# Key decay on VectorE, silu in one ScalarE instruction, and another order of products and out-stages in a decoder layer

## The chip, the cores and the metric

One core of a Trainium2 chip runs one launch of the kernel. The metric is the device time in microseconds (us), the median of several runs. The engines work on their own instruction queues, in order, and wait for each other on semaphores: PE (TensorE, matmuls), ACT (ScalarE), DVE (VectorE), POOL (GpSimd) and SP (SyncE, which issues most DMAs).

## What is computed

A decoder layer with batch 2, 512 tokens, width 1024: linear attention with 32 heads of 128, a quantised product with a context, and a blocked feed-forward part, each with a residual and a layer norm. The change touches the attention alone:

```python
qkv = jax.nn.silu(hidden_states @ qkv_w.T)
...
scores = jnp.einsum('bhnd,bhmd->bhnm', cq, ck) * diag_decay
intra = jnp.einsum('bhnm,bhmd->bhnd', scores, cv)
inter = jnp.einsum('bhnd,bhde->bhne', cq * q_decay, kv)
kv_next = kv * block_decay + jnp.einsum('bhnd,bhne->bhde', ck * k_decay, cv)
...
gate = jax.nn.sigmoid(hidden_states @ gate_w.T)
return gate * normed @ out_w.T
```

## The kernel before

`make_plan` writes one list of steps; each engine's program walks this list and emits its own part of every step. So the order of the list is the order of every engine's queue, and nothing is reordered later.

Heads go in pairs, n = 0 to 15. For n = 1 to 14 one iteration of `main_part` holds four projections, in the order gate, q, k, v. Each is a `product_pair`: a block scheme with seven products (1 to 7) instead of eight, each of 12 matmuls of 128x512. Every fp32 operand is held as two f16 parts, high and low, and a product takes three terms (hi*hi, hi*lo, lo*hi: lines 1386, 1387, 1388). The high part is written by ACT, the low part by DVE (`split_low`, line 1740). The four results r of a projection come from bank 0 (product 2), bank 1 (product 3), bank 2 (product 4), and `p_copy` (products 5 and 7, joined by the addition `c22`, line 1791). `u3` (line 1788) joins products 6 and 7 in bank 2 ahead of products 4 and 5; product 3 waits for `c22`; `seed` (line 1617) copies bank 0 into bank 1 ahead of product 2.

Between the products, `slots` put other work: `p6` is what follows product 6. There are the splits of the next weights (`part(0)`, `part(1)`, `part(2)`: ACT line 1601, DVE line 1740), whose sums POOL makes (`pair_sum`, lines 2026 to 2031: the sum `s1` feeds part 1, `s4` part 2); the attention of the pair before (`scores`, `attend`, `gated`); and its output projection, 16 `out_stage` steps (`stages`), also in seven products, of three matmuls each (lines 1473 to 1475), whose results DVE adds into `acc` (line 1908). Stages 0 to 3 stand in q, 4 to 11 in k, 12 to 15 in v. Stage 1 needs the block `S2`, a sum of gated units that POOL makes and ACT (line 1671) and DVE split into `gated_split`.

A `silu` step is: ACT Sigmoid into `sig` (line 1637), DVE multiply of result and `sig` (line 1801), ACT high part (line 1643), DVE low part. For the keys, results 0 and 2 are kept in `sig`; POOL multiplies them by the decay (`k_decay`, line 2047) once the low part is done; `turn_keys` splits them and SP transposes them by DMA, for the `state` product (line 1359) at the start of the next gate. The values are transposed by DMA as well (`v_turn`); their result 0 goes through the buffer `s_kt` (named `scores_keys` in the profile), which the scores' split writes as well.

## Time and profile before

| | us |
|---|---|
| median of 3 runs | 1957.35 (1956.63 to 1958.7) |
| the profiled execution, its own time | 1958.86 |
| its span in the profile | 1957.0 |
| PE busy in the span | 1804.3 |
| DVE busy | 1474.8 |
| ACT busy | 927.7 |
| POOL busy | 705.5 |

The span runs from the first to the last instruction of one execution; its own time is 1.9 us longer. Matmuls are pipelined, so that the busy time of PE counts overlapping instructions once; where it waits, the profile shows idle time and what ended it.

### The profile page before, as it was taken

To read this page: it belongs to the slowest core of one execution; us is meant where nothing else is said; L and a number is where in the kernel's file an instruction comes from. 1 tells how busy PE (TensorE), PEld (TensorE's weight loads), DVE (VectorE), ACT (ScalarE), POOL (GpSimd) and SP (SyncE) were. 2 spreads that over 40 slices of the span, in tenths; PEclk is the share of its full clock that TensorE was granted. 3 is DMA by queue.
4 is the path that set the end of the run, shared out by engine and by line. 5 is a ranking of instruction groups with operands and counts; after the bars stand their busy time and mean duration, and the time that the engine had idled before them with its cause. 6 is when DMAs were issued, how large, how long until landed. Compare 5 with 4: busy or idle time off the path is not lost.

```text
span 1957.0 us, 27828 instructions
## 1 busy us (share of the span) xinstructions
PE 1804.3 (92%) x9865; PEld 892.1 (46%) x9865; DVE 1474.8 (75%) x2029; ACT 927.7 (47%) x1402; POOL 705.5 (36%) x536
## 2 busy tenths in 40 slices
PE   7899899999999999999999998999999998998887
PEld 4354434445454544435454444445453444565332
DVE  7777777868777777878776777868677777768877
ACT  5554444545454444545444444445444454434674
POOL 3253333344433343344333333444333433301433
PEclk9999999999999999999999999999999999999998
DMA  5223323131423223131321213131231313233322
GB/s 183 61 65 99 69 87 102 65 102 44 129 60 97 71 87 102 61 102 49 114 75 58 78 54 83 51 93 56 70 69 50 103 54 81 76 100 116 108 87 87
DMA packets 158119, 161.54 MB, mean 83 GB/s; under 512 B 99872, under 2 KB 127904, under 8 KB 157600
## 3 DMA queue, kind: packets, MB, share of 16 engines
q1 hardware_dynamic: 146528, 147.09, 25.6%
q0 software_dynamic: 2560, 8.39, 1.3%
q10 hardware_dynamic: 8896, 4.28, 0.8%
q8 instruction: 82, 1.34, 0.3%
q14 instruction: 53, 0.43, 0.1%
HBM read 123.56 MB, written 12.58 MB: 70 GB/s over the span
## 4 chain that ended last, share of the span: by engine, by line
DVE 42%; PE 19%; issue 13%; ACT 12%; DMA 9%; POOL 4%; SPq 1%; ACTq 0%; DVEq 0%; POOLq 0%
DVE w_pair L1740 7%; DVE acc L1908 5%; DVE gated_split L1740 5%; DVE scores_keys L1740 4%; PE bank L1386 4%; PE bank L1387 4%; PE bank L1388 4%; DMA decay_sb<-rates 3%; DMA v_split<-scores_keys 3%; DVE w_vo L1740 3%; DVE bank L1801 3%; PE bank L1359 3%; ACT w_pair L1601 3%; ACT sig L1637 2%; DVE p_copy L1791 2%
## 5 line engine op out<-in xcount | busy, mean ns | idle before, releaser
L1386 PE MATMUL bank<-x_blocks,w_pair 128*128 128x512 f16 (+1 forms) x1820 | 684.8, 376 | 33.0 <-DVE p_copy L1791 17.6
L1387 PE MATMUL bank<-x_blocks,w_pair 128*128 128x512 f16 (+1 forms) x1820 | 683.5, 376 | 0.0
L1388 PE MATMUL bank<-x_blocks,w_pair 128*128 128x512 f16 (+1 forms) x1820 | 682.4, 375 | 0.0
L1386 PEld LDWEIGHTS bank<-x_blocks,w_pair 128*128 128x128 f16 x1820 | 179.4, 99 | 246.6 <-DVE p_copy L1791 24.8
L1388 PEld LDWEIGHTS bank<-x_blocks,w_pair 128*128 128x128 f16 x1820 | 179.4, 99 | 206.8 <-issue 7.2
L1387 PEld LDWEIGHTS bank<-x_blocks,w_pair 128*128 128x128 f16 x1820 | 179.4, 99 | 190.5 <-issue 7.0
L1740 DVE SCALAR_TENSOR_TENSOR w_pair<-raw_pair,w_pair 128x1024 f16<-128x1024 f32 x126 | 183.4, 1475 | 54.4 <-ACT w_pair L1601 54.2
L1908 DVE TENSOR_TENSOR acc<-acc,bank 128x512 f32<-128x512 f32 x320 | 206.6, 677 | 13.9 <-PE bank L1475 13.9
L2047 POOL TENSOR_TENSOR sig<-sig,decay_sb 128x512 f32<-128x512 f32 x30 | 38.2, 1272 | 474.2 <-DVE k_units L1740 474.2
L1473 PE MATMUL bank<-w_vo,gated_split 128*128 128x512 f16 x392 | 151.6, 387 | 62.0 <-DVE acc L1908 47.9
L2057 POOL TENSOR_TENSOR ssq<-ssq,sig 128x512 f32<-128x512 f32 x64 | 81.9, 1279 | 268.7 <-ACT sig L1659 268.7
L1475 PE MATMUL bank<-w_vo,gated_split 128*128 128x512 f16 x392 | 151.6, 387 | 0.0
L1474 PE MATMUL bank<-w_vo,gated_split 128*128 128x512 f16 x392 | 151.2, 386 | 0.0
L1740 DVE SCALAR_TENSOR_TENSOR scores_keys<-bank,scores_keys 128x256 f16<-128x256 f32 (+1 forms) x176 | 89.1, 543 | 81.0 <-ACT scores_keys L1651 42.0
L1601 ACT ACTIVATE w_pair<-raw_pair 128x1024 f16<-128x1024 f32 x126 | 129.1, 1049 | 43.6 <-POOL raw_pair L2027 43.6
L2026 POOL TENSOR_TENSOR sums_pair<-raw_pair 128x512 f32<-128x512 f32 x63 | 100.8, 1600 | 113.3 <-DVE w_pair L1740 93.7
L1637 ACT ACTIVATE sig<-bank 128x512 f32<-128x512 f32 x145 | 85.8, 592 | 114.0 <-PE bank L1388 74.0
L1740 DVE SCALAR_TENSOR_TENSOR gated_split<-k_units,gated_split 128x512 f16<-128x512 f32 x98 | 123.3, 1269 | 9.7 <-ACT gated_split L1671 9.7
L1740 DVE SCALAR_TENSOR_TENSOR w_pair<-sums_pair,w_pair 128x1536 f16<-128x1536 f32 x63 | 110.4, 1753 | 1.9 <-ACT w_pair L1601 0.7
L1651 ACT ACTIVATE scores_keys<-bank 128x512 f16<-128x512 f32 (+1 forms) x132 | 58.6, 491 | 111.8 <-DMA v_split<-scores_keys 74.7
L1659 ACT ACTIVATE sig<-bank 128x512 f32<-128x512 f32 x64 | 38.2, 597 | 149.1 <-DVE bank L1879 147.0
L1601 ACT ACTIVATE w_pair<-sums_pair 128x1536 f16<-128x1536 f32 x63 | 93.0, 1475 | 30.0 <-POOL sums_pair L2031 30.0
(220 smaller groups left out, 2849.6 us busy)
## 6 DMA issues: line engine op xcount, KB each, us to landing
raw_pair<-w_qk SPq DMA_DIRECT2D x32, 1024.0 KB, 5.6
raw_pair<-w_gate SPq DMA_DIRECT2D x16, 1024.0 KB, 5.0
raw_pair<-w_out SPq DMA_DIRECT2D x16, 1024.0 KB, 5.1
raw_pair<-w_vt SPq DMA_DIRECT2D x15, 1024.0 KB, 4.9
raw_pair<-ctx_in SPq DMA_DIRECT2D x8, 1024.0 KB, 4.9
decay_sb<-rates SPq DMA_DIRECT2D x60, 128.0 KB, 4.5
acc<-x_t SPq DMA_DIRECT2D x4, 1024.0 KB, 11.2
ctx<-raw_pair SPq DMA_DIRECT2D x8, 512.0 KB, 3.9
```

The costliest lines, as they stand in the source:

```text
L1386: pe.matmul(out, w_hi, x_hi, start=unmet and k == 0, stop=False, skip_group_check=halves or not fresh)
L1387: pe.matmul(out, w_hi, x_lo, start=False, stop=False, skip_group_check=halves or not fresh)
L1388: mm = pe.matmul(out, w_lo, x_hi, start=False, stop=k == QT - 1, skip_group_check=halves or not fresh)
L1473: pe.matmul(out, g_hi, w_hi, start=fresh, stop=False, skip_group_check=not fresh)
L1474: pe.matmul(out, g_hi, w_lo, start=False, stop=False, skip_group_check=not fresh)
L1475: pe.matmul(out, g_lo, w_hi, start=False, stop=True, skip_group_check=not fresh).then_inc(sem["out_mm"])
L1601: act.activation(hi, src, ACT.Copy, scale=W_SCALE).then_inc(sem["w_hi"])
L1637: act.activation(c.sig32[st["gi"]][:, :], src, ACT.Sigmoid, scale=st["sign"] / W_SCALE).then_inc(sem["sig"])
L1740: return dve.scalar_tensor_tensor(out=lo, in0=src, scalar=scale, in1=hi, op0=ALU.mult, op1=ALU.subtract)
L1908: dve.tensor_tensor(dst, dst, bank, ALU.add).then_inc(sem["acc"])
L2026: pool.tensor_tensor(s3, a11, a21, ALU.add)
L2057: pool.tensor_tensor(c.ssq[:, b], c.ssq[:, b], c.sig32[st["gi"]][:, :], ALU.add).then_inc(sem["ssq"])
```

## The change

1. The decay of the keys, `k_decay`, is made by DVE instead of POOL, and stands in the list as a step of its own: `decay(0)` in k between `stages(8)` and `part(1)`, `decay(1)` after `part(0)` at the end of k.
2. `silu` is one ACT instruction, `ACT.Silu`, from the bank into `sig`; both splits read `sig`; DVE's multiply is gone. A bank is released once ACT has read it. Gate keeps Sigmoid.
3. In q, product 7 stands ahead of 6, `gate(3)` and `gate(2)` come right behind the last attention, the q result of product 2 behind stage 0, and unit 3 and `S2` are split behind it. In v, the order is 1, 7, 6, 4, 2, 5, 3, the stages 14 and 15 stand behind 6 and 4, and the scores behind 5. The values' result 2, made by product 4, goes through `s_kt` in place of result 0.

```diff
@@ -85,7 +85,7 @@
 FIRST = {
     "before": "x0 v0 t1 v1 l x2 p00 t3 p10 x1 p11 p01 x3 w0 t2 p02 w2 p12 x5 p03",
     "q": {"p1": "x6 x4 w1 e00", "p7": "l", "p6": "w0 w1 p13 w2", "p4": "l", "p3": "w0"},
-    "k": {"p1": "e10", "p6": "w1 w2 l", "p5": "j0", "p3": "c w0 j1"},
+    "k": {"p1": "e10", "p6": "w1 w2 l d0", "p5": "j0", "p3": "d1 c w0 j1"},
     "gate": {"p2": "e01 e11", "p6": "s0", "p5": "g0", "p4": "w1 w2", "p3": "l g2 g3 g1"},
 }
...
@@ -326,33 +326,29 @@
         self.gate_done[r // 2] = self.tick("gate_sig")
         self.release(place, self.gate_done[r // 2])
-    def silu(self, done, place, sign, dst, dst_free, kept=False):
+    def silu(self, done, place, sign, dst, dst_free):
         gi = self.sig_at % 2
         self.sig_at += 1
-        st = self.add("silu", done=done, place=place, sign=sign, gi=gi, sig_free=self.sig_free[gi], sig=self.tick("sig"),
-                      silu=self.tick("silu"), dst=dst, free=dst_free if isinstance(dst_free, list) else [dst_free],
-                      slot=self.late_slot, hi=self.tick("qkv_hi"), kept=kept)
-        self.sig_free[gi] = st["silu"]
-        self.kept = gi, st["silu"]
-        return self.tick("qkv_lo")
+        st = self.add("silu", done=done, place=place, sign=sign, gi=gi, sig_free=self.sig_free[gi], silu=self.tick("silu"),
+                      dst=dst, free=dst_free if isinstance(dst_free, list) else [dst_free], slot=self.late_slot,
+                      hi=self.tick("qkv_hi"))
+        lo = self.sig_free[gi] = self.tick("qkv_lo")
+        return gi, st["silu"], lo
     def qk_out(self, which, r):
         done, place, sign = self.result(r)
-        decayed = which == "k" and r % 2 == 0
-        lo = self.silu(done, place, sign, (which, r), [self.qk_free, self.g_split] if which == "k" else
-                       [self.qk_free, self.q_read], decayed)
-        if decayed:
-            gi, silu = self.kept
-            self.release(place, silu)
-            self.decay_keys(r // 2, gi, lo)
-        else:
-            self.release(place, lo)
+        gi, silu, lo = self.silu(done, place, sign, (which, r), [self.qk_free, self.g_split] if which == "k" else
+                                 [self.qk_free, self.q_read])
+        self.release(place, silu)
+        if which == "k" and r % 2 == 0:
+            self.kd[r // 2] = gi, lo
         for b in range(B):
             self.qk_done[(which, r // 2, b)] = lo
-    def decay_keys(self, g, gi, lo):
+    def decay_keys(self, g):
+        gi, lo = self.kd[g]
         self.add("k_decay", g=g, gi=gi, lo=lo, rate=self.rate_ready[g])
         rate = self.rate_free[g] = self.sig_free[gi] = self.tick("k_rate")
         self.kd[g] = gi, rate
...
@@ -387,11 +383,11 @@
     def v_out(self, r):
         done, place, sign = self.result(r)
-        lo = self.silu(done, place, sign, ("v_unit", r), self.s_free if r == 0 else self.vo_free)
-        self.release(place, lo)
+        _, silu, lo = self.silu(done, place, sign, ("v_unit", r), self.s_free if r == 2 else self.vo_free)
+        self.release(place, silu)
         self.add("v_turn", r=r, ready=lo, free=max(self.v_hl_free))
         self.v_turned[r] = self.tick(f"v_turned{r}", 16)
-        if r == 0:
+        if r == 2:
             self.s_free = self.v_turned[r]
         if r == 1:
             self.v_done = [[self.v_turned[2:], self.v_turned[:2]] for _ in range(B)]
...
@@ -806,7 +802,7 @@
             plan.add_c22()
         if i in (6, 7) and {6, 7} <= met:
             plan.add_u3()
-        if i in (2, 5, 4, 3):
+        if i in (2, 5, 4, 3) and i not in put_off:
             out({2: 0, 5: 3, 4: 2, 3: 1}[i])
         fill(f"p{i}")
...
@@ -962,12 +961,12 @@
             "p4": [part(1)],
             "p3": [part(2)],
         } if last else {
-            "p1": [attend(3), gated(3)] + units(3),
-            "p2": sums(S2) + split_sum(S2) + stages(0) + sums(S1),
-            "p6": stages(1) + split_sum(S1) + sums(S4) + gate_rest + split_sum(S4),
-            "p7": stages(2) + [part(0), part(1)],
+            "p1": [attend(3), gated(3)] + gate_rest,
+            "p2": sums(S2) + stages(0) + [lambda: plan.qk_out("q", 0)] + units(3) + split_sum(S2) + sums(S1),
+            "p7": stages(1) + split_sum(S1) + sums(S4) + split_sum(S4),
+            "p6": stages(2) + [part(0), part(1)],
             "p3": stages(3) + [part(2)],
-        }, (1, 2, 6, 7, 5, 4, 3))
+        }, (1, 2, 6, 7, 5, 4, 3) if last else (1, 2, 7, 6, 5, 4, 3), put_off=() if last else (2,))
         plan.load_decay(n * GH, last)
         plan.load_decay(n * GH + 1, last)
         if last:
...
@@ -977,18 +976,19 @@
             "p1": stages(4) + stages(5) + ([stash] if stashing else []),
             "p7": stages(6),
             "p2": stages(7),
-            "p6": [part(0)] + stages(8) + [part(1)] + stages(9),
+            "p6": [part(0)] + stages(8) + [decay(0), part(1)] + stages(9),
             "p5": stages(10) + [part(2)] + [turn(0)],
             "p4": stages(11),
-            "p3": [part(0)],
+            "p3": [part(0), decay(1)],
         })
         plan.load_rates(n, "q")
         product_pair(plan, "v", n, {
             "p1": stages(12) + [turn(1), part(1)],
             "p7": stages(13) + [part(2)],
-            "p2": stages(14),
-            "p6": stages(15) + [lambda: plan.scores(n, UNITS[0])],
-        }, (1, 7, 2, 6, 4, 5, 3))
+            "p6": stages(14),
+            "p4": stages(15),
+            "p5": [lambda: plan.scores(n, UNITS[0])],
+        }, (1, 7, 6, 4, 2, 5, 3))
 def final_part(plan):
...
@@ -1631,12 +1631,12 @@
             until(act, sem, st["free"])
             act.activation(c.sig32[st["gi"]][:, :], c.banks[st["bank"]][:, :], ACT.Copy).then_inc(sem["v_copied"])
         elif kind == "silu":
-            src = c.placed(st["place"])
             act.wait_ge(sem[st["done"][0]], st["done"][1])
             until(act, sem, st["sig_free"])
-            act.activation(c.sig32[st["gi"]][:, :], src, ACT.Sigmoid, scale=st["sign"] / W_SCALE).then_inc(sem["sig"])
+            act.activation(c.sig32[st["gi"]][:, :], c.placed(st["place"]), ACT.Silu,
+                           scale=st["sign"] / W_SCALE).then_inc(sem["silu"])
+            src = c.sig32[st["gi"]][:, :]
             act.wait_ge(sem["silu"], st["silu"][1])
-            src = c.sig32[st["gi"]][:, :] if st["kept"] else src
             for token in st["free"]:
                 until(act, sem, token)
             for cols, (dst, _) in c.split_targets(st):
...
@@ -1795,12 +1795,7 @@
             dve.wait_ge(sem["v_mm"], st["mm"][1])
             dve.tensor_tensor(bank[:, :], c.sig32[st["gi"]][:, :], bank[:, :], ALU.subtract).then_inc(sem["v_sub"])
         elif kind == "silu":
-            src = c.placed(st["place"])
-            dve.wait_ge(sem["sig"], st["sig"][1])
-            out = c.sig32[st["gi"]][:, :] if st["kept"] else src
-            dve.scalar_tensor_tensor(out=out, in0=src, scalar=st["sign"] / W_SCALE, in1=c.sig32[st["gi"]][:, :],
-                                     op0=ALU.mult, op1=ALU.mult).then_inc(sem["silu"])
-            src = out
+            src = c.sig32[st["gi"]][:, :]
             dve.wait_ge(sem["qkv_hi"], st["hi"][1])
             for cols, (hi, lo) in c.split_targets(st):
                 ins = split_low(like(src[:, cols], lo), 1.0, hi, lo)
...
@@ -1859,6 +1854,11 @@
+        elif kind == "k_decay":
+            k = c.sig32[st["gi"]][:, :].rearrange("p (b s) -> p b s", b=B)
+            dve.wait_ge(sem["qkv_lo"], st["lo"][1])
+            until(dve, sem, st["rate"])
+            dve.tensor_tensor(k, k, c.rate(st["g"], B), ALU.mult).then_inc(sem["k_rate"])
```

What this does to the queues, at three places. ACT at the start of q: the rows of before, then of the changed kernel. `k_units` holds the gated units here, `p_copy` and the banks the gate results. L1671 splits a unit or sum, L1676 is the seed of an out-stage.

```order
-L1637 ACTIVATE sig_0<-bank 128x512
-L1643 ACTIVATE q_units<-bank 128x2x256
-L1671 ACTIVATE gated_split<-k_units 128x512
-L1676 ACTIVATE bank<-bank 128x512
-L1671 ACTIVATE gated_split<-k_units 128x512
-L1627 ACTIVATE gate_units<-p_copy 128x2x256
-L1627 ACTIVATE gate_units<-bank 128x2x256
```

```order
+L1627 ACTIVATE gate_units<-p_copy 128x2x256
+L1627 ACTIVATE gate_units<-bank 128x2x256
+L1676 ACTIVATE bank<-bank 128x512
+L1636 ACT_TABLE_LOAD
+L1636 ACTIVATE sig_0<-bank 128x512
+L1643 ACTIVATE q_units<-sig_0 128x2x256
+L1671 ACTIVATE gated_split<-k_units 128x512 x2
```

Both gate results and the seed moved ahead, a table load stands before the first silu of q, and the splits of unit 3 and `S2` moved behind it. The other load of an iteration stands ahead of `gate(0)`.

POOL in k, before: four sums of a weight pair (here the k weights'), the decay, and the sums of the v weights, then the second decay.

```order
L2031 TENSOR_TENSOR sums_pair<-raw_pair,sums_pair 128x512
L2047 TENSOR_TENSOR sig_0<-sig_0,decay_sb 128x512
L2026 TENSOR_TENSOR sums_pair<-raw_pair 128x512
L2027 TENSOR_TENSOR raw_pair<-raw_pair 128x512
L2029 TENSOR_TENSOR sums_pair<-raw_pair 128x512
L2031 TENSOR_TENSOR sums_pair<-raw_pair,sums_pair 128x512
L2047 TENSOR_TENSOR sig_0<-sig_0,decay_sb 128x512
```

In the changed kernel the two rows with `decay_sb` are gone from POOL and the sums follow each other. DVE in k has the first of them, now line 1861, between the splits of `part(0)` and `part(1)`:

```order
L1788 TENSOR_TENSOR bank<-bank,p_copy 128x512
L1740 SCALAR_TENSOR_TENSOR w_pair<-raw_pair,w_pair 128x1024
L1908 TENSOR_TENSOR acc<-acc,bank 128x512
L1861 TENSOR_TENSOR sig_0<-sig_0,decay_sb 128x512
L1740 SCALAR_TENSOR_TENSOR w_pair<-raw_pair,w_pair 128x1024
L1908 TENSOR_TENSOR acc<-acc,bank 128x512 x2
L1791 TENSOR_TENSOR p_copy<-bank,p_copy 128x512
```

Before, the same rows stood there without the line 1861.

## Rows read from the trace of the kernel before

**Rows 1.** The page, busy time of each engine over the span.

```profile
PE 1804.3 (92%) x9865; PEld 892.1 (46%) x9865; DVE 1474.8 (75%) x2029; ACT 927.7 (47%) x1402; POOL 705.5 (36%) x536
```

**Rows 2.** The waits of PE: us in total, times, longest.

```profile
PE bank L1473 <- DVE acc L1908: 47.9, 40, 2.6
PE bank L1386 <- DVE p_copy L1791: 17.6, 14, 2.6
```

**Rows 3.** Windows: length, busy us of PE, PEld, DVE, ACT, POOL, then clock, DMA.

```profile
599.50:660.66 61.16, 56.36 (x256) 24.54 (x255) 44.14 (x57) 26.89 (x38) 20.59 (x14) 0.97 0.40 112
660.66:688.37 27.71, 27.71 (x205) 17.18 (x205) 23.02 (x34) 15.15 (x25) 10.04 (x8) 1.00 0.18 48
688.37:710.09 21.72, 20.60 (x96) 8.79 (x94) 17.45 (x23) 10.62 (x18) 11.41 (x8) 1.00 0.14 49
```

**Rows 4.** Timeline of PE: last product of v, first product and state of gate.

```profile
654.52 0.39 PE L1386 MATMUL bank<-x_blocks,w_pair 128*128 128x512 f16 x1 [0.92 <-DVE p_copy L1791]
654.74 0.38 PE L1387 MATMUL bank<-x_blocks,w_pair 128*128 128x512 f16 x1
...
660.66 0.83 PE L1359 MATMUL bank<-v_split,scores_keys 128*128 128x128 f16 x12 [0.79 <-DMA v_split<-w_vo]
```

**Rows 5.** Timeline: the stall in the k product, 604 to 627 us; its first and last kin.

```profile
177.93 0.39 PE L1473 MATMUL bank<-w_vo,gated_split 128*128 128x512 f16 x1 [2.59 <-DVE acc L1905]
...
604.27 0.37 SPq L1319 DMA_DIRECT2D raw_pair<-w_vt  x1
614.38 1.28 POOL L2047 TENSOR_TENSOR sig<-sig,decay_sb 128x512 f32<-128x512 f32 x1 [22.81 <-DVE k_units L1740]
619.18 1.06 ACT L1601 ACTIVATE w_pair<-raw_pair 128x1024 f16<-128x1024 f32 x1 [3.12 <-POOL raw_pair L2027]
621.44 1.27 DVE L1908 TENSOR_TENSOR acc<-acc,bank 128x512 f32<-128x512 f32 x2
622.77 0.39 PE L1473 MATMUL bank<-w_vo,gated_split 128*128 128x512 f16 x1 [2.60 <-DVE acc L1908]
...
623.75 0.63 PE L1473 MATMUL bank<-w_vo,gated_split 128*128 128x512 f16 x1
...
626.31 0.48 PE L1386 MATMUL bank<-x_blocks,w_pair 128*128 128x512 f16 x1
...
1621.29 0.39 PE L1473 MATMUL bank<-w_vo,gated_split 128*128 128x512 f16 x1 [2.59 <-DVE acc L1908]
```

**Rows 6.** The page, DMA issues: KB each, median us to landing.

```profile
raw_pair<-w_vt SPq DMA_DIRECT2D x15, 1024.0 KB, 4.9
```

**Rows 7.** Timeline of DVE, ACT, POOL and PE, end of gate to q.

```profile
680.65 0.68 DVE L1740 SCALAR_TENSOR_TENSOR gated_split<-k_units,gated_split 128x512 f16<-128x512 f32 x1
...
690.23 0.75 DVE L1888 SCALAR_TENSOR_TENSOR k_units<-bank,norm_w_sb,gate_units 128x512 f32<-128x512 f32 x1 [0.75 <-ACT sig L1659]
...
691.50 4.36 POOL L2053 TENSOR_TENSOR k_units<-k_units 128x512 f32<-128x512 f32 x3
...
695.21 1.21 DVE L1740 SCALAR_TENSOR_TENSOR gated_split<-k_units,gated_split 128x512 f16<-128x512 f32 x1
695.63 0.39 PE L1473 MATMUL bank<-w_vo,gated_split 128*128 128x512 f16 x1 [0.62 <-ACT bank L1676]
```

**Rows 8.** Groups of DVE instructions: busy us, mean ns, idle before.

```profile
L1801 DVE SCALAR_TENSOR_TENSOR bank<-bank,sig 128x512 f32<-128x512 f32 x115 | 79.5, 691 | 17.8 <-ACT sig L1637 17.7
L1801 DVE SCALAR_TENSOR_TENSOR p_copy<-p_copy,sig 128x512 f32<-128x512 f32 x47 | 33.6, 714 | 32.7 <-ACT sig L1637 32.7
L1801 DVE SCALAR_TENSOR_TENSOR sig<-bank,sig 128x512 f32<-128x512 f32 x30 | 20.7, 692 | 47.4 <-ACT sig L1637 47.4
```

**Rows 9.** Timeline of ACT around a table load, product q of block 0.

```profile
38.89 1.04 ACT L1601 ACTIVATE w_pair<-raw_pair 128x1024 f16<-128x1024 f32 x1
39.95 1.28 ACT L1637 ACT_TABLE_LOAD   x1
41.25 0.60 ACT L1637 ACTIVATE sig<-bank 128x512 f32<-128x512 f32 x1
```

More of the change, by code:

```diff
@@ L66 @@
 SEMAPHORES = (
-    ["const_in", "ones_set", "constants", "quant_set", "x_hi", "x_lo", "w_hi", "w_lo", "sig", "silu", "qkv_hi", "qkv_lo",
+    ["const_in", "ones_set", "constants", "quant_set", "x_hi", "x_lo", "w_hi", "w_lo", "silu", "qkv_hi", "qkv_lo",
      "gate_sig", "score_mm", "decayed", "s_hi", "s_lo", "attend_mm", "sq", "gated", "g_sum", "g_hi", "g_lo", "ssq", "out_mm", "out_seeded",
@@ L250, in split_vo @@
         self.add("vo_split", part=part, slot=item["slot"], ready=item["landed"], late=late, out=item["what"][0] == "o",
-                 free=[max(self.first_mm.values())] if late else [self.vo_free] + self.v_turned[1:], hi=self.tick("w_hi"))
+                 free=[max(self.first_mm.values())] if late else [self.vo_free, self.v_turned[0], self.v_turned[1], self.v_turned[3]], hi=self.tick("w_hi"))
         lo = self.tick("w_lo")
@@ L270, in split_wo @@
         ready = (item["t1"], item["t1"], item["t4"])[part]
-        self.add("wo_split", part=part, slot=item["slot"], ready=ready, free=[self.vo_free] + self.v_turned[1:],
+        self.add("wo_split", part=part, slot=item["slot"], ready=ready, free=[self.vo_free, self.v_turned[0], self.v_turned[1], self.v_turned[3]],
                  hi=self.tick("w_hi"))
@@ L378, in kv_out @@
         done, place, sign = self.result(r)
-        lo = self.silu(done, place, sign, ("kv", b, r), [self.qk_free, self.g_split, self.late_units_free])
-        self.release(place, lo)
+        _, silu, lo = self.silu(done, place, sign, ("kv", b, r), [self.qk_free, self.g_split, self.late_units_free])
+        self.release(place, silu)
         self.qk_done[("k", r // 2, b)] = lo
@@ L424, in end_v @@
         bank = v["banks"][half]
-        done = self.silu(v["mm"][half], bank, 1.0, ("v", v["b"], half), self.v_hl_free[v["b"]])
+        _, silu, done = self.silu(v["mm"][half], bank, 1.0, ("v", v["b"], half), self.v_hl_free[v["b"]])
         self.v_done[v["b"]] = [[done]] * GH
-        self.main_ring.give(bank, done)
+        self.main_ring.give(bank, silu)
     def values(self, b):
@@ L929, in state, with decay @@
             return lambda: plan.state(g)
+        def decay(g):
+            return lambda: plan.decay_keys(g)
         def turn(g):
@@ L1160, in __init__ @@
         self.g32 = {unit: k_flat[:, unit * D:(unit + 1) * D].bitcast(F32) for unit in UNITS}
-        self.v_units = [self.s_kt[:, 0:2 * S]]
-        self.v_units += [vo_flat[:, i * 2 * S:(i + 1) * 2 * S] for i in range(3)]
+        self.v_units = {r: vo_flat[:, i * 2 * S:(i + 1) * 2 * S] for i, r in enumerate((0, 1, 3))}
+        self.v_units[2] = self.s_kt[:, 0:2 * S]
         self.hid += [self.g[:, i].rearrange("p n s -> p (n s)").bitcast(F32) for i in range(4)]
```

11 lines of the change are left out of this document (3 added, 8 removed).

## The prediction

> **What bounds the kernel now.** I read the busy times first. PE works 1804 of 1957 us, DVE 1475 [rows 1], so TensorE is the engine to keep fed, and DVE the one that most often fails to feed it. The waits of PE say where: out-products wait for DVE's additions into `acc` (47.9 us in 40 waits, the longest 2.6), and products for DVE's `c22` addition (17.6 us) [rows 2]. Everything repeats with n, 14 times (n = 1 to 14), so I cut one iteration into stretches: from the first product of k to the first product of the next gate 61.16 us, the rest of gate with its attention 27.71 us, and q up to its last out-product 21.72 us, together 110.6 us [rows 3]. The gate stretch has PE busy all through.
>
> How much of the other two is stall? Two products start 0.22 us apart when nothing waits (654.52 and 654.74 [rows 4]); I use 0.216. The k/v stretch holds 15 products of 12 and 21 out-products of 3 matmuls, 243 x 0.216 = 52.5 us, and 12 short score matmuls (2304 columns in each of their three terms' sum, about 1.0 us): 53.5 of 61.2, so 7.7 us per iteration are stalls and slow matmuls. The q stretch holds 72 + 21 matmuls, 20.1 of 21.7 us: 1.6 us of stalls.
>
> The large stall is that of the out-stage behind product 5 of k: PE waits 2.60 us for `acc` at 622.77, and the same stands at 177.93 first and 1621.29 last, once in each of the 14 iterations [rows 5]. Followed back: the addition (621.44) stands on DVE behind the low split of the v weights' part 1; that waits for ScalarE's high split (619.18), which waited 3.12 us for POOL's sum `raw_pair` L2027. POOL was late because it works in program order and the k decay (614.38) stood ahead of the sums: it had waited 22.81 us for the split of the keys, then took 1.28 us. The v weights had been asked for at 604.27; such a load lands in 4.9 us, at 609.2 [rows 5, 6]. POOL lost 6.4 us (609.2 to 615.66) that nothing in the data required.
>
> Behind this stall the matmuls last 0.63 instead of 0.38 us (623.75, still 0.48 at 626.31 [rows 5]), and the granted clock of the stretch reads 0.97 while the other two have 1.00 [rows 3]: the engine fell from 2.4 to 1.2 GHz for some eight matmuls after idling 2.6 us, 8 x 0.21 = 1.7 us. Two smaller waits end the stretch: product 3 of v 0.92 us for `c22`, the state product 0.79 us for the transposed values [rows 4].
>
> **The change, part by part.**
>
> *Decay to DVE.* Removes the POOL instruction above; POOL's sums can start at landing. In the times of the trace: sums from 609.2, each 1.28 alone, so s1 at 611.8 and s4 at 614.4, ahead of every user. ScalarE's part 1 then follows part 0 and the seed, at 616.1 to 617.2, instead of 620.2. DVE: `u3` to 615.5, part 0 to 616.7, one addition to 617.4, the decay to 618.1 (no row shows it on DVE; the two-input split of the same shape is 0.68 with POOL idle, 1.21 beside POOL [rows 7]; POOL is idle here, so 0.7), part 1 to 619.3, two additions to 620.5. PE is ready at 620.2 (622.77 less its wait): the stall shrinks from 2.6 to 0.5, and the half-clock matmuls go. The second decay frees POOL the same way for the sums of the gate weights. These sums feed the splits behind which the additions of stage 13 stand, on which stage 14 waits. Of the 47.9 us in [rows 2] 13 waits of 2.6 are the stall above (the first of the 14 waited for a copy, L1905); the other 27 share 14 us, 1 us per iteration, and should mostly go.
>
> *Silu in one instruction.* Removes DVE's multiply: 115 + 47 + 30 = 192 instructions, 133.8 us of DVE [rows 8], 0.7 us from the chain of each of the 12 results per iteration, and with it a handshake ScalarE to DVE and back. ScalarE's own count stays; Silu is in no row; Sigmoid of this shape is 0.60 (41.25 [rows 9]) and so is Square, whose end starts gated at 690.23 [rows 7]. An activation of 1024 columns lasts 1.04 [rows 9], so 512 columns lie between half of that and 0.60: I take 0.60. But the low split now reads `sig` in SBUF instead of a bank: 0.68 alone, 1.21 beside POOL [rows 7]. POOL is busy a third of the time [rows 1], so of 12 splits some 4 lose 0.5 us: 8.4 saved and about 2 + 2 x 0.7 given back, net 5 us of DVE per iteration.
>
> *Table loads.* Gate still uses Sigmoid, so each iteration loads a table twice: ahead of gate(0) and ahead of the first q silu, 30 more in all. The trace shows one between two activations: previous end 39.93, load 39.95 to 41.23, next 41.25 [rows 9]: 1.28 us plus the 0.1 by which activations otherwise overlap, 1.38. The Trainium skill (ScalarE: Activation LUTs, What ACT_TABLE_LOAD costs) prices a switch at 1.28 us of load and 1.38 us of drain, 2.66 in all; this row shows no such drain, and I go by the row. By the skill's figure each of the two places would be some 1.3 us later and the time 1926 + 14 x 2.6 = 1962 us.
>
> *v products reordered, scores behind product 5.* The scores (1.0 us of PE) now stand between product 5 and product 3, which waits for `c22`: that covers the 0.92 us. Also the values that go through the scores' buffer come from product 4 before the scores, and their transpose is over when the scores are split; ScalarE no longer stands behind it. New risk: product 4 follows product 6 with one out-stage between (1.3 us), and `u3` on DVE stands behind stage 13's additions and a 1.75 us split; I work out 0.6 us of stall. The state product needs v's transposes; their chain is a multiply and a handshake shorter (about 0.75 us) and PE arrives sooner: 0.3 us of wait left.
> Sum for k/v: 0.5 + 0.6 + 0.3 and 0.3 of small seed waits = 1.7 us of stall against 7.7: gain 6.0. Low end: only the 2.6 us stall and the `c22` wait go, 3.5; high end 7.
>
> *q reordered.* Here the change costs. Cut the chain at the last attend of the iteration, whose matmuls end at 688.37. First, the load ahead of gate(0) sits in front of the split of S3 and of an out-weight part, for which DVE works without slack, so DVE's join and ScalarE's work reach attend 3 about 1.3 us later; the seed of q then ends at 689.2 and product 2, ahead of which it had half a us to spare, starts 0.9 us late. gated(3), 690.23 to 690.98 [rows 7], becomes 692.3. ScalarE next has gate(3), gate(2), the out seed (3 x 0.6, to 694.0), the load, silu and high split of q (2.6, to 696.5); only then the high splits of unit 3 and of S2. DVE behind it: low splits of q, unit 3 and S2. In the trace such a split beside POOL lasts 1.21 (695.21, POOL busy from 691.50 [rows 7]), and POOL will be busy: 3 x 1.21, to 700.1. PE arrives at S2's product at 696.4 (product 2, stage 0, product 7, three matmuls). Stall 3.7 us; with 0.68 per split it is 2.1. Before, S2 was ready at 696.4, and PE stalled 0.62 there (695.63). So stalls of 3.7 + 0.9 = 4.6 against 1.6: loss 3.0. What follows (`u3`, stage 2, the splits) I find covered. And a 3.7 us idle may drop the clock as the 2.6 us one does, 1.7 us; it did so in part of the iterations, so I charge half, 0.8.
>
> **Sum.** 6.0 - 3.0 - 0.8 = 2.2 us per iteration, 14 x 2.2 = 31 us; start and end, with 2 loads and a few shorter chains, about nothing. The profiled execution took 1958.9 us with a span of 1957.0; the median of the runs is 1957.35, which the forecast starts from: 1926 us.
>
> **Rivals.**
> - *S2's split decides (slower).* Place: stage 1 of q. The row shows a load behind an idle-free copy, not one between PSUM reads of other tables. Bounded from above by two loads' length in each place (2 x 1.28), and with the clock dropping each time, the loss is 3.0 + 2 x 1.28 + 1.7 = 7.3 against 6.0: +1.3 x 14 = +18, 1975 us. It decides from a loss of 6 us per iteration in q. For it: a load and three splits in a row ahead of one product. Against: the gap of 0.02 us behind the load [rows 9]. Chance 0.2. (The Trainium skill's drain, cited above, is this mechanism.)
> - *The gain stays at the stall itself.* DVE is busy 44 of 61 us in the stretch [rows 3]; if the next stall takes over there (stage 14, or product 4 behind `u3`), k/v gains 3.5, all that q costs (3.8): 1957 to 1961. Chance 0.15.
> - *q is cheap.* Splits at 0.68 and the gate's load absorbed: the stall at S2 is 1.7, no more than q has now; no clock drop: 14 x 5.9 = 83, 1875 us. Against: POOL works all through that place. Chance 0.2.
> - *My sum*, own range 1905 to 1945: chance 0.45.
>
> **How the numbers follow.** A measurement of this kernel tells some 0.2% (4 us) from no change. Faster: 0.45 + 0.2 and a part of the second rival, 0.7. Same 0.08. Slower 0.22. The range leaves out half of the cheap case's far end and half of the slow one's: 1882 to 1970.
>
> **What would show it.** Right: the 2.6 us waits of out-products for `acc` in k are gone; POOL's sums begin at landing; DVE's busy time falls by about 70 to 100 us; no wait of product 3 of v; a new wait of PE in q for the low split of `gated_split`, 2 to 4 us, 14 times; table loads of 1.28 us. Wrong: if that q wait is above 6 us or absent, or if the k stall remains with another releaser (then the late sums were not its cause). The forecast fails most easily in q, where I placed eight instructions from durations taken in another order.

## The result: 16 us faster, half of what was forecast

| | before | after |
|---|---|---|
| median, us | 1957.72 (4 runs) | 1941.45 (1940.58 to 1946.51, 4 runs) |
| ratio, 95% interval | | 0.9922 (0.9905 to 0.994) |
| profiled execution, its span | 1958.86, 1957.0 | 1941.43, 1939.6 |

The forecast was 1926 us, a gain of 31; 1941.45 lies in its range of 1882 to 1970, and the gain of 16 is about half of it.

The page of the profile after, busy time of each engine, to be set beside [rows 1]:

```profile
PE 1808.5 (93%) x9865; PEld 896.1 (46%) x9865; DVE 1383.3 (71%) x1867; ACT 975.0 (50%) x1432; POOL 641.9 (33%) x506
```

DVE has 91.5 us less to do, ACT 47 us more, most of it the 30 table loads (30 x 1.28 = 38). PE has the same matmuls and is busy 4 us longer although the span is 17 us shorter: some of them have become slow. The waits of PE (total, times, longest), to be set beside [rows 2]:

```profile
PE bank L1473 <- issue: 54.5, 14, 3.9
PE bank L1386 <- DVE bank L1788: 12.1, 15, 0.8
...
PE bank L1386 <- ACT gate_units L1627: 5.0, 12, 0.4
...
PE bank L1359 <- DVE k_units L1888: 4.7, 12, 0.4
...
PE bank L1473 <- DVE acc L1908: 0.6, 3, 0.2
```

The two rows of before have all but gone: out-products wait 0.6 us in all for this addition into `acc`, never more than 0.2, and `c22` holds up one product in all. In their place stands one wait, 14 times 3.9 us. "issue" means that no releaser is shown; the timeline finds it below. The three stretches of one iteration, cut as in [rows 3] but in time order k/v, gate, q:

```profile
595.72:651.19 55.47, 54.47 (x257) 24.18 (x256) 40.49 (x49) 26.36 (x37) 16.14 (x12) 1.00 0.41 123
651.19:679.56 28.37, 27.97 (x204) 17.09 (x205) 22.60 (x33) 17.01 (x26) 10.03 (x8) 1.00 0.20 48
679.56:707.27 27.71, 23.37 (x96) 9.66 (x95) 16.14 (x21) 12.21 (x19) 11.24 (x8) 0.88 0.11 39
```

k/v gave 5.7 us (61.16 before), gate lost 0.7 (27.71), q lost 6.0 (21.72). The clock reads 1.00 where it was 0.97, and 0.88 in q, where it was 1.00.

**k.** POOL, DVE and PE in the timeline, where [rows 5] had the 2.60 us stall:

```profile
604.68 1.27 POOL L2026 TENSOR_TENSOR sums_pair<-raw_pair 128x512 f32<-128x512 f32 x1 [21.22 <-DMA raw_pair<-w_vt]
...
613.35 0.69 DVE L1861 TENSOR_TENSOR sig<-sig,decay_sb 128x512 f32<-128x512 f32 x1
613.95 1.22 DVE L1740 SCALAR_TENSOR_TENSOR w_pair<-raw_pair,w_pair 128x1024 f16<-128x1024 f32 x1
615.09 1.28 DVE L1908 TENSOR_TENSOR acc<-acc,bank 128x512 f32<-128x512 f32 x2
...
616.42 0.39 PE L1473 MATMUL bank<-w_vo,gated_split 128*128 128x512 f16 x1
```

POOL's first sum now waits for its load (DMA), no longer for a decay; the decay costs DVE 0.69 us; the out-stage starts without a wait.

**q.** ACT, DVE, POOL and PE of the same iteration:

```profile
684.49 1.28 ACT L1636 ACT_TABLE_LOAD   x1
685.78 0.60 ACT L1636 ACTIVATE sig<-bank 128x512 f32<-128x512 f32 x1
686.41 0.63 ACT L1643 ACTIVATE q_units<-sig 128x512 f16<-128x512 f32 x1
686.95 1.13 ACT L1671 ACTIVATE gated_split<-k_units 128x512 f16<-128x512 f32 x2
...
687.07 0.85 DVE L1740 SCALAR_TENSOR_TENSOR q_units<-sig,q_units 128x512 f16<-128x512 f32 x1 [2.73 <-ACT q_units L1643]
687.85 3.42 DVE L1740 SCALAR_TENSOR_TENSOR gated_split<-k_units,gated_split 128x512 f16<-128x512 f32 x2
...
687.34 1.71 POOL L2026 TENSOR_TENSOR sums_pair<-raw_pair 128x512 f32<-128x512 f32 x1
...
687.07 0.38 PE L1475 MATMUL bank<-w_vo,gated_split 128*128 128x512 f16 x1
691.38 0.58 PE L1473 MATMUL bank<-w_vo,gated_split 128*128 128x512 f16 x1 [3.92 <-issue]
...
692.61 0.63 PE L1386 MATMUL bank<-x_blocks,w_pair 128*128 128x512 f16 x1
693.03 0.63 PE L1387 MATMUL bank<-x_blocks,w_pair 128*128 128x512 f16 x1
```

DVE idled 2.73 us for the chain load, silu, high split. Then it made the low splits of q, of unit 3 and of `S2`, the last two at 1.7 us each with POOL at work (whose own sum lasts 1.71 instead of 1.27). They end at 691.27 and PE goes on at 691.38. Between the last start before the wait and the first behind it lie 4.31 us, 4.08 to 4.09 more than between neighbours. The profile itself gives the idle time, 3.92; a "stall" below is counted between starts, a "wait" in the profile's rows is idle time. Behind it the matmuls start 0.42 us apart (692.61, 693.03) instead of 0.216: the lower clock level, 1.2 GHz, for 13 matmuls here.

### The profile page after: what moved, and what is told of

Its sections match the earlier page's. It is cut to its first block, busy times and chain, and to the rows that moved or that the text cites. A ratio compares the mean times of both kernels' runs of the same rounds, so it can differ in the third digit from the quotient of the medians.

```text
span 1939.6 us, 27666 instructions
## 1 busy us (share of the span) xinstructions
PE 1808.5 (93%) x9865; PEld 896.1 (46%) x9865; DVE 1383.3 (71%) x1867; ACT 975.0 (50%) x1432; POOL 641.9 (33%) x506
## 4 chain that ended last, share of the span: by engine, by line
PE 54%; DVE 17%; issue 16%; ACT 9%; POOL 3%; DMA 1%; ACTq 0%; DVEq 0%; POOLq 0%; SPq 0%
PE bank L1386 13%; PE bank L1387 13%; PE bank L1388 13%; DVE w_pair L1740 4%; PE bank L1359 4%; PE bank L1473 3%; PE bank L1475 3%; PE bank L1474 2%; DVE acc L1908 2%; POOL ssq L2052 1%; ACT sig L1636 1%; DVE gated_split L1740 1%; ACT k_units L1643 1%; ACT w_pair L1601 1%; PE bank L1537 1%
## 5 line engine op out<-in xcount | busy, mean ns | idle before, releaser
L2026 POOL TENSOR_TENSOR sums_pair<-raw_pair 128x512 f32<-128x512 f32 x63 | 93.5, 1485 | 647.8 <-DVE w_pair L1740 453.5
L1908 DVE TENSOR_TENSOR acc<-acc,bank 128x512 f32<-128x512 f32 x320 | 212.0, 681 | 43.6 <-PE bank L1475 41.9
L1740 DVE SCALAR_TENSOR_TENSOR w_pair<-raw_pair,w_pair 128x1024 f16<-128x1024 f32 x126 | 170.2, 1370 | 14.0 <-ACT w_pair L1601 13.9
L1636 ACT ACTIVATE sig<-p_copy 128x512 f32<-128x512 f32 x47 | 29.6, 630 | 244.7 <-DVE p_copy L1791 244.7
L1740 DVE SCALAR_TENSOR_TENSOR k_units<-sig,k_units 128x512 f16<-128x512 f32 (+1 forms) x68 | 69.9, 1027 | 101.0 <-ACT k_units L1643 90.6
L1740 DVE SCALAR_TENSOR_TENSOR q_units<-sig,q_units 128x512 f16<-128x512 f32 x64 | 49.3, 770 | 100.8 <-ACT q_units L1643 100.8
L1740 DVE SCALAR_TENSOR_TENSOR gated_split<-k_units,gated_split 128x512 f16<-128x512 f32 x98 | 111.9, 1164 | 10.9 <-ACT gated_split L1671 10.9
L1740 DVE SCALAR_TENSOR_TENSOR w_pair<-sums_pair,w_pair 128x1536 f16<-128x1536 f32 x63 | 110.5, 1755 | 5.1 <-ACT w_pair L1601 3.8
L1740 DVE SCALAR_TENSOR_TENSOR scores_keys<-bank,scores_keys 128x256 f16<-128x256 f32 (+1 forms) x162 | 79.5, 532 | 42.6 <-ACT scores_keys L1666 22.7
```

Source lines behind the costliest of these rows:

```text
L1636: act.activation(c.sig32[st["gi"]][:, :], c.placed(st["place"]), ACT.Silu, scale=st["sign"] / W_SCALE).then_inc(sem["silu"])
L1740: return dve.scalar_tensor_tensor(out=lo, in0=src, scalar=scale, in1=hi, op0=ALU.mult, op1=ALU.subtract)
L1908: dve.tensor_tensor(dst, dst, bank, ALU.add).then_inc(sem["acc"])
L2026: pool.tensor_tensor(s3, a11, a21, ALU.add)
```

## Experiments

The first four ran beside each other (before: 1958.24 us), the next four (1958.01), then the last two (1959.21). "Changed" is the changed kernel. Where an edit adds or removes a source line, line numbers move by one to six. A line `...` stands for parts of an edit that are left out.

**decay_only.** Before, with the decay alone moved to DVE, at the two places of the change.

```diff
-            self.decay_keys(r // 2, gi, lo)
+            self.kd[r // 2] = gi, lo
...
-            "p6": [part(0)] + stages(8) + [part(1)] + stages(9),
+            "p6": [part(0)] + stages(8) + [lambda: plan.decay_keys(0), part(1)] + stages(9),
...
-            "p3": [part(0)],
+            "p3": [part(0), lambda: plan.decay_keys(1)],
...
```

> The kernel before with one edit: the decay of the keys on DVE, at the places it has in the changed kernel; silu, gate, q and v as before. Theory of the late sums (the prediction's): POOL's sums start when the v weights land, the 2.6 us wait of the out-stage behind product 5 of k falls to 0.7 us or less in all 14 iterations, and so do the half-clock matmuls behind it: 1925 us, between 1915 and 1935. Rival (DVE's load is the bound, the late sums only the place where it shows): the wait moves to the next additions, 1950 to 1958 us, DVE busy 20 us more.

Measured: 1914.23 us (1911.32 to 1916.01), ratio 0.9781 (0.9765 to 0.9798). The waits of PE:

```profile
PE bank L1474 <- DVE acc L1914: 18.0, 41, 0.7
PE bank L1387 <- DVE p_copy L1792: 16.2, 14, 2.5
```

The longest wait for `acc` fell from 2.6 to 0.7 us, the wait for `c22` stayed. One part of the change gives 44 us, more than twice what the whole gives. It is 11 us more than I expected, 1 us outside the range; from the first iteration to the last the timeline holds no half-clock matmuls, where before has 80 (17 us).

**q_split_first.** Changed, with unit 3 and `S2` split ahead of q's first result and its table load; all loads stay.

```diff
-            "p1": [attend(3), gated(3)] + gate_rest,
-            "p2": sums(S2) + stages(0) + [lambda: plan.qk_out("q", 0)] + units(3) + split_sum(S2) + sums(S1),
+            "p1": [attend(3), gated(3)] + gate_rest + units(3),
+            "p2": sums(S2) + split_sum(S2) + stages(0) + sums(S1) + [lambda: plan.qk_out("q", 0)],
```

> The changed kernel with one edit in q: the splits of unit 3 and S2 stand ahead of the out seed, and the q result of product 2 (with the table load) behind them. Theory of the order in q: the 4.1 us wait of the S2 out-product falls to 1 us or less, and with it the matmuls at half clock behind it (8 to 13 of them, 1.7 to 2.8 us): 4 to 6 us per iteration, 1941 to 1857 to 1885 us. Rival (something else holds the iteration at 110.4 us, for example the weight loads and POOL's sums, so that PE waits elsewhere): 1925 us or more, with a new wait in k or v of the size of the one removed.

Measured: 1891.68 us (1887.85 to 1892.65), ratio 0.9659 (0.964 to 0.9678). The waits of PE:

```profile
PE bank L1386 <- DVE bank L1788: 23.1, 29, 0.8
PE bank L1473 <- DVE acc L1908: 13.6, 15, 1.0
```

The 3.9 us wait and every half-clock matmul of the iterations are gone: 50 us by the place of two steps. It is 7 us short of the expected range. The 14 iterations alone gave 56 us, 4.0 each, the low end of what I expected, since two waits follow: stage 2 now waits 1.0 us for `acc`, behind the q split and its load, and product 5 waits 0.8 us for `u3` in q, as a product in v does. Start and end together took 6 us more than in the changed kernel's profile.

**gate_silu.** Changed, with gate through Silu too, so that no table is switched in an iteration. Its gate values are not the reference's.

```diff
-            act.activation(dst, like(c.placed(st["place"]), dst), ACT.Sigmoid,
+            act.activation(dst, like(c.placed(st["place"]), dst), ACT.Silu,
```

> The changed kernel with the gate computed by the Silu function instead of Sigmoid (so the gate values are others than the reference's), which leaves no table load in the loop; everything else is the same. Theory that both loads lie on the chain to S2: the wait of the S2 out-product falls from 4.1 to about 1.5 us, the seed of q is 1.3 us earlier, together 2.7 us per iteration and part of the half-clock matmuls: 1890 to 1905 us. Rival (the loads are hidden and only the order of the splits counts): 1935 to 1941 us. If a switch costs the 2.66 us that the Trainium skill states (ScalarE: Activation LUTs, What ACT_TABLE_LOAD costs), the wait would vanish altogether and ACT's idle time would fall by as much again as its loads.

Measured: 1896.85 us (1894.38 to 1899.2), ratio 0.9693 (0.9674 to 0.9713). The waits of PE:

```profile
PE bank L1473 <- issue: 34.9, 14, 2.5
```

Two loads (2.6 us of ACT) per iteration are worth 45 us, 3.2 per iteration, in this order: 1.4 us of the `S2` wait, the gate's waits, and 89 of 126 half-clock matmuls (89 x 0.21 = 19 us). These stand behind only 5 of the 14 waits now, 7 or 8 at a time; in the other 9 iterations a new stall of 0.74 us for `u3` in q takes a part back.

**multiply_back.** Changed, with Sigmoid and DVE's multiply again: no loads in an iteration, and 192 multiplies. The product always goes into `sig` in SBUF, so that the splits read `sig` as in the changed kernel, not a bank as before.

```diff
...
-            act.activation(c.sig32[st["gi"]][:, :], c.placed(st["place"]), ACT.Silu,
+            act.activation(c.sig32[st["gi"]][:, :], c.placed(st["place"]), ACT.Sigmoid,
...
+            dve.wait_ge(sem["sig"], st["sig"][1])
+            dve.scalar_tensor_tensor(out=src, in0=c.placed(st["place"]), scalar=st["sign"] / W_SCALE, in1=src,
+                                     op0=ALU.mult, op1=ALU.mult).then_inc(sem["silu"])
...
```

> The changed kernel with silu undone alone: Sigmoid by ScalarE into sig, DVE's multiply of the result and sig into sig; the decay on DVE and all orders stay as changed, no table loads in the loop. DVE gets 192 multiplies of 0.69 us back (133 us). Theory (silu's gain on DVE is mostly hidden in this order, its loads are not): the wait for S2 loses 1.4 us of load and gains about 0.8 us of multiply and handshake, the gate part gains 1.3 us: 1920 to 1935 us, faster than the changed kernel. Rival (the single-instruction silu is where the gain came from): 1960 us or more.

Measured: 1970.37 us (1964.36 to 1975.52), ratio 1.0058 (1.0034 to 1.0082). The waits of PE, then DVE in q:

```profile
PE bank L1473 <- issue: 55.0, 14, 3.9
PE bank L1473 <- DVE acc L1911: 17.1, 27, 0.8
...
PE bank L1359 <- DMA v_split<-w_vo: 11.2, 14, 1.0
```

```profile
698.94 0.69 DVE L1800 SCALAR_TENSOR_TENSOR sig<-bank,sig 128x512 f32<-128x512 f32 x1
700.32 1.53 DVE L1740 SCALAR_TENSOR_TENSOR q_units<-sig,q_units 128x512 f16<-128x512 f32 x1 [0.69 <-ACT q_units L1643]
701.78 3.42 DVE L1740 SCALAR_TENSOR_TENSOR gated_split<-k_units,gated_split 128x512 f16<-128x512 f32 x2
```

My expectation fell, and the time is the rival's. The chain to `S2` lost the load's 1.28 us and got the multiply (0.69) and a q split of 1.53 instead of 0.85: the same wait. So Silu with its loads is worth 29 us in this order and 74 without them (gate_silu), and what a load costs depends on what would stand in its place in that chain.

**decay_back.** Changed, with the decay on POOL again, right behind the key result.

```diff
             self.kd[r // 2] = gi, lo
+            self.decay_keys(r // 2)
...
-            "p6": [part(0)] + stages(8) + [decay(0), part(1)] + stages(9),
+            "p6": [part(0)] + stages(8) + [part(1)] + stages(9),
...
```

> The changed kernel with the decay alone undone: it runs on POOL again, directly behind the key result, as before. Theory of the late sums: POOL's sums of the v weights wait for the keys again, PE waits 2 to 3 us for acc behind product 5 of k in every iteration, with half-clock matmuls behind it: 2.5 to 4 us per iteration, 1975 to 1995 us. Rival (in the new order the sums have slack, and the move was worth something only before): 1941 to 1950 us.

Measured: 2016.03 us (2009.53 to 2020.6), ratio 1.0303 (1.028 to 1.0325). Its timeline, POOL, ACT and PE in k:

```profile
745.51 1.27 POOL L2043 TENSOR_TENSOR sig<-sig,decay_sb 128x512 f32<-128x512 f32 x1 [27.27 <-DVE k_units L1741]
750.30 1.06 ACT L1602 ACTIVATE w_pair<-raw_pair 128x1024 f16<-128x1024 f32 x1 [2.39 <-POOL raw_pair L2023]
...
753.89 0.39 PE L1474 MATMUL bank<-w_vo,gated_split 128*128 128x512 f16 x1 [1.86 <-DVE acc L1904]
```

The chain of [rows 5] is back link by link, with late sums; its wait is 1.9 us, less than the 2 to 3 expected, and no half-clock matmuls stand behind it. With it come waits in v of up to 2.4 us for `u3` (33.9 us in 16, start included), and half-clock matmuls behind these and behind the wait for `S2`. The decay is worth 75 us in this order, 21 more than I expected at most.

**v_back.** Changed, with the order of v (products, stages, scores, and the values' buffer) as before.

```diff
...
-            "p6": stages(14),
-            "p4": stages(15),
-            "p5": [lambda: plan.scores(n, UNITS[0])],
-        }, (1, 7, 6, 4, 2, 5, 3))
+            "p2": stages(14),
+            "p6": stages(15) + [lambda: plan.scores(n, UNITS[0])],
+        }, (1, 7, 2, 6, 4, 5, 3))
...
```

> The changed kernel with v alone undone: products in the order 1, 7, 2, 6, 4, 5, 3, stages 14 and 15 and the scores behind 2 and 6, result 0 through the scores' buffer. Theory: the waits of product 3 for c22 (0.9 us) and of the state product for the transposes (0.8 us, less 0.7 for the shorter chain) return, and the 0.97 us wait of product 4 for u3 goes: +0 to +1 us per iteration, 1941 to 1955 us. Rival (the order of v carries the gain of k and v): 1970 us or more.

Measured: 1949.1 us (1947.23 to 1949.67), ratio 0.9951 (0.9935 to 0.9968). The wait of product 3 for `c22` is back (16.0 us in 15 waits). The new order of v is worth 8 us, as expected.

**q_back.** Changed, with the order of q as before. Its results are then read in two groups with gate's between them, so that it loads four tables per iteration instead of two.

```diff
-            "p1": [attend(3), gated(3)] + gate_rest,
-            "p2": sums(S2) + stages(0) + [lambda: plan.qk_out("q", 0)] + units(3) + split_sum(S2) + sums(S1),
-            "p7": stages(1) + split_sum(S1) + sums(S4) + split_sum(S4),
-            "p6": stages(2) + [part(0), part(1)],
+            "p1": [attend(3), gated(3)] + units(3),
+            "p2": sums(S2) + split_sum(S2) + stages(0) + sums(S1),
+            "p6": stages(1) + split_sum(S1) + sums(S4) + gate_rest + split_sum(S4),
+            "p7": stages(2) + [part(0), part(1)],
...
-        }, (1, 2, 6, 7, 5, 4, 3) if last else (1, 2, 7, 6, 5, 4, 3), put_off=() if last else (2,))
+        }, (1, 2, 6, 7, 5, 4, 3))
```

> The changed kernel with q alone undone: products 1, 2, 6, 7, 5, 4, 3, S2 split ahead of stage 0, gate(3) and gate(2) behind stage 1. That puts Sigmoid between silus, so an iteration loads a table four times, not twice (58 loads in the loop). Theory (order, not loads, makes the long stall): the 4.1 us wait and its half-clock matmuls go (6.5 us), two more loads of 1.38 us and the old waits of q (1.6 us) come, at worst all in PE's way: 1941 - 14 x 6.5 + 14 x 4.4 = 1911 us, between 1885 and 1925. Rival (loads are what costs): 1950 us or more.

Measured: 1894.59 us (1890.82 to 1895.74), ratio 0.9677 (0.9661 to 0.9693). The page and the waits:

```profile
PE 1787.4 (95%) x9865; PEld 888.1 (47%) x9865; DVE 1393.1 (74%) x1867; ACT 1012.8 (54%) x1460; POOL 647.6 (34%) x506
```

```profile
PE bank L1386 <- DVE bank L1788: 14.9, 29, 0.8
PE bank L1473 <- ACT bank L1676: 10.7, 13, 0.9
PE bank L1473 <- issue: 9.4, 14, 0.7
PE bank L1386 <- ACT gate_units L1627: 9.4, 14, 0.7
```

With twice the loads (ACT 38 us busier) it is 47 us faster than the changed kernel, inside the expected range, and has no half-clock matmuls in the iterations. The new order of q is the one part of the change that costs, and it costs 47 us.

**u3_first.** q_split_first, with two DVE splits moved behind `u3`: S4's in q, and the gate weights' last part in v.

```diff
-            "p7": stages(1) + split_sum(S1) + sums(S4) + split_sum(S4),
-            "p6": stages(2) + [part(0), part(1)],
+            "p7": stages(1) + split_sum(S1) + sums(S4),
+            "p6": split_sum(S4) + stages(2) + [part(0), part(1)],
...
-            "p7": stages(13) + [part(2)],
-            "p6": stages(14),
+            "p7": stages(13),
+            "p6": [part(2)] + stages(14),
```

> q_split_first with two more moves: the split of S4 behind u3 in q, and part(2) of the gate weights behind u3 in v. Both u3 additions are then the next thing DVE does when product 6 ends; PE waits 0.95 and 0.97 us for them in every iteration of q_split_first. Theory (each wait is local): 1.5 to 1.9 us less per iteration, 1892 to 1866 to 1873 us. Rival (106.65 us per iteration, which q_split_first and gate_silu share to 0.05 us, is set by a chain beside PE): the waits move, 1886 to 1892 us.

Measured: 1859.73 us (1857.03 to 1861.57), ratio 0.9495 (0.9479 to 0.9511). The waits for `u3` went. The 14 iterations gave 27.1 us, which is the two waits of 0.96 us x 14; the other 4 to 5 us lie outside the iterations, and take the total 6 us below the expected range.

**units_first.** Changed, with only unit 3's split moved ahead of q's first result; `S2`'s stays behind it.

```diff
-            "p1": [attend(3), gated(3)] + gate_rest,
-            "p2": sums(S2) + stages(0) + [lambda: plan.qk_out("q", 0)] + units(3) + split_sum(S2) + sums(S1),
+            "p1": [attend(3), gated(3)] + gate_rest + units(3),
+            "p2": sums(S2) + stages(0) + [lambda: plan.qk_out("q", 0)] + split_sum(S2) + sums(S1),
```

> The changed kernel with only the split of the last gated unit moved ahead of the gate results, so that it no longer waits behind the Silu load; S2's own split stays behind q's first result. My theory: stage 1's wait shrinks from 4.08 us to between 2 and 3 us, and what the shorter stall saves is its own 1 to 2 us in each iteration and, on top, part of the half-clock matmuls behind it, since stalls of 2.7 us had them in 5 to 9 of 14 places and stalls of 4.08 us in 13 of 14: 1941 - 14 x (1.5 + 0.8) = 1909 us, 1897 to 1922. Rival: the clock has no part in it and only the wait counts, 1941 - 14 x 1.5 = 1920 us, with as many half-clock places as before. Second rival: the Silu load ahead of q's first split sets the end of the wait anyway, stall of 3.5 us or more and 1932 us or above.

Measured: 1918.38 us (1917.17 to 1919.87), ratio 0.9792 (0.9776 to 0.9809). The wait of stage 1 in the timeline of PE:

```profile
682.34 0.38 PE L1473 MATMUL bank<-w_vo,gated_split 128*128 128x512 f16 x1 [2.64 <-issue]
682.55 0.38 PE L1474 MATMUL bank<-w_vo,gated_split 128*128 128x512 f16 x1
```

The total lies by the first rival (1920), but by the accounts of the next section its condition is not met: from the first state product to the last, the 14 iterations took 1516.27 us against 1546.35, 30.1 less. The wait went from 4.08 to 2.80 us: 14 x 1.28 = 17.9. Half-clock matmuls went from 126 to 62: 64 x 0.211 = 13.5. Together 31.4. Waits that moved with them bring it to 30.0: `u3` in q is waited for in 5 iterations (0.74 us each, 3.7 more), and the two stalls of 0.56 and 0.58 us at attend 3 and at bank 2 come in 2 iterations fewer (2.3 less). The 7 us by which the whole fell short lie outside the iterations (400.3 us of the span against 393.3), where the edit changes nothing; 8 half-clock matmuls at 57 us, which the changed kernel's profile does not have there, are 1.7 of them.

**loads_later.** u3_first, with both loads of an iteration behind the work that PE waits for.

```diff
-            "p4": sums(S3) + [gate(0)] + split_sum(S3) + [wo(1), attend(2), score(3), gated(2)],
+            "p4": sums(S3) + split_sum(S3) + [wo(1), gate(0), attend(2), score(3), gated(2)],
...
-            "p2": sums(S2) + split_sum(S2) + stages(0) + sums(S1) + [lambda: plan.qk_out("q", 0)],
-            "p7": stages(1) + split_sum(S1) + sums(S4),
+            "p2": sums(S2) + split_sum(S2) + stages(0) + sums(S1),
+            "p7": stages(1) + split_sum(S1) + [lambda: plan.qk_out("q", 0)] + sums(S4),
```

> The fastest version so far (1859.7 us) with both table loads of an iteration moved behind the work that the matmuls wait for: q's first result (and its Silu load) behind stages 1 and S1's split, and the gate's first result (and its Sigmoid load) behind S3's split and the next weight part. My theory: stage 2's wait for the accumulator falls from 1.18 us to about 0.4, and the two waits of 0.55 and 0.58 us at attend 3 and at the gate's bank shrink or stay: 1859.7 - 14 x (0.8 to 1.6) = 1837 to 1849 us. Rival: a result that is read later gives its bank back later, and the wait moves to a later product of the same pair: 1857 us or above.

Measured: 1834.02 us (1833.36 to 1837.04), ratio 0.936 (0.9345 to 0.9376), the fastest of all. The page, then what is left of waits in products:

```profile
PE 1776.7 (97%) x9865; PEld 892.8 (49%) x9865; DVE 1375.3 (75%) x1867; ACT 976.3 (53%) x1432; POOL 656.1 (36%) x506
```

```profile
PE bank L1386 <- DVE bank L1788: 3.4, 12, 0.8
```

The waits for `acc`, for the gate's bank and for attend 3 are gone; an iteration takes 102.6 us on average, against 110.5. The loads are all still there, and PE hardly waits for them: of the gaps, one of 0.34 us is left in most iterations. The total is 3 us below the expected range.

## Why the prediction was right in direction and twice too large

Each profile is cut in three here; the middle part runs from the first state product of a gate (line 1359) to the fifteenth, 14 iterations apart; half-clock matmuls are those that start 0.42 us after the one before:

| | before the first | 14 iterations | behind the last | half-clock matmuls in the 14 |
|---|---|---|---|---|
| before | 105.29 | 1553.74 | 297.97 | 80, at 11 places |
| after | 100.61 | 1546.35 | 292.64 | 126, at 13 places |
| units_first | 102.23 | 1516.27 | 298.1 | 62, at 9 places |
| gate_silu | 100.53 | 1497.89 | 294.08 | 37, at 5 places |
| decay_only | 102.48 | 1507.29 | 299.7 | none |
| q_back | 102.42 | 1495.3 | 291.28 | none |

The iterations gave 7.4 us where 31 were forecast; start and end, which I put at nothing, gave 10.0. Of the 7.4, the first iteration gave 4.9 (111.84 to 106.96 us) and the other 13 together 2.5 (1441.90 to 1439.39). So the place where the forecast put its whole gain, the repeated iteration, gave next to nothing. That the total came out on the forecast's side, and at half of it, is in good part luck.

- *Decay to DVE: right.* Stall 2.60 to none (0.5 forecast), decay 0.69 (0.7). Decay_only and decay_back are this step done and undone, 44 and 75 us.
- *Silu in one instruction: right.* 0.60 us each, DVE 91.5 us less (70 to 100 forecast).
- *Table loads: right.* The load lasted 1.28 us, from 684.49 to 685.77, and the next activation began at 685.78. The Trainium skill's drain of 1.38 us (ScalarE: Activation LUTs, What ACT_TABLE_LOAD costs) is not there: the copy ahead of the load (line 1676) ended at 684.47.
- *v: right in sum.* The wait for `c22` gone; 0.97 us for `u3` (0.6 forecast), none for the state product (0.3). In the iteration of the windows k/v gained 5.7 us against 6.0.
- *q's stalls: the right places, a little small.* 4.08 us at `S2` (3.7), 0.55 and 0.58 at attend 3 and at bank 2 (0.9 at product 2): 5.2 against 4.6, which is 0.6 x 14 = 8 us. The splits I had at 1.21 lasted 1.7.
- *The clock: the step that failed.* "It did so in part of the iterations, so I charge half, 0.8." It came behind 13 of the 14 stalls, and where it came it lasted up to 13 matmuls, not eight: 126 x 0.211 / 14 = 1.9 us per iteration. The missing 1.1 x 14 = 15 us, with the 8 of the stalls, are about the 24 us by which the iterations fell short. Two smaller terms nearly cancel: k/v's missing 0.3 is 4 us more, and the 110.59 us that I took for every iteration of before [rows 3] were 110.98 on average, 5 us more to gain. Three of those iterations last 112.60 to 112.75 us, because product 3 of v waited 2.25 to 2.62 us for `c22` in them, not the 0.92 of [rows 4], with 7 or 8 half-clock matmuls behind it.
- *Start and end: "about nothing" was wrong too*, by 10 us the other way. Before, PE waited 1.75 and 2.06 us at 89.9 and 92.5, with 11 half-clock matmuls behind, and 2.14, 0.96 and 0.70 us in the last gate, q and attention (1715.8, 1740.4, 1771.9); after, 2.42 us at 56.9 stands for the first two, and the others are down to 0.67, 0.29 and 0.46 us. How much of it recurs is open: among the versions of the table the end alone varies by 8 us.

The clock term is the one that was mis-sized most. That it acts on the time is seen where the stall is the same and the number of half-clock matmuls differs. In the changed kernel, behind the same stall of 4.09 us, iterations with 11 to 13 of them take 111.2 to 111.6 us and most of those with 5 to 8 take 109.9 to 110.4 (one takes 109.2, without the two small stalls at attend 3 and bank 2): six matmuls more, 6 x 0.211 = 1.3 us more. In multiply_back, at the same stall, the last two iterations have none and take 109.27 and 109.07 us, those with 12 or 13 take 112.0 to 112.7 (some small waits differ there too). Units_first fits too, with 30.0 of its 30.1 us accounted for.

In before, the slow matmuls behind the stall of k cost nothing. The six iterations that have them there and nowhere else last 110.08 to 110.49 us, the four without any 110.37 to 110.41. With them, the out-stage behind product 2 of v, 19.6 us later, finds its addition nearly done; without them it waits. The first row below is from an iteration with them, the second from one without:

```profile
642.38 0.39 PE L1473 MATMUL bank<-w_vo,gated_split 128*128 128x512 f16 x1 [0.27 <-DVE acc L1908]
...
752.93 0.39 PE L1473 MATMUL bank<-w_vo,gated_split 128*128 128x512 f16 x1 [1.87 <-DVE acc L1908]
```

After the change nothing is waited for behind them, and they cost what they last.

Of the rivals, the one that S2's split decides had the right place and put the loss in q at 7.3 us per iteration, the forecast at 3.8. Measured are 5.2 - 1.6 + 1.9 = 5.5, halfway between, and just under the 6 us from which that rival decides; in the iteration of the windows, with its 13 half-clock matmuls, gate and q together lost 6.7 us and k/v gained 5.7. Its clock term, 1.7 us each time, was the better one (1.9 measured). Its other term, loads dearer than 1.28 us, was not found: the next activation began 0.01 us behind the load. The two other rivals fell: k/v gained more than 3.5 us, and q was not cheap.

By parts, from the medians: decay 44 us, Silu and v's order another 20 (decay_only against q_back), q's order minus 47. That is one order of undoing them; decay_back, in another, puts the decay at 75. It is not the forecast's own split either: I set the new q against the old q of before, while q_back is the old order with Silu and four loads, which has waits of its own (its rows above).

## What to carry to other kernels

When a change takes a load off an engine and reorders work too, price each reordering by what stands ahead of the first instruction that TensorE waits for; a table load of 1.28 us shortened that wait by 1.4 us when it went (gate_silu), and moved behind it was hardly waited for (loads_later). A stall long enough to drop the clock costs more than its length, and how much more depends on whether the engine would have waited behind it anyway (nothing in k of before, all of it in q after). Undo each part alone before judging the whole: here one part gave 44 us and another took 47.
